# A two-layer macaron block on one core: later k products, weight blocks one a turn, a bias by a product, norms on VectorE at the joins

## The reference, cut to what matters

```python
def ffn0(x):                      # ternary weights
    h = relu(einsum('bsd,fd->bsf', x, quantize(W1)) + b1)       # width 512
    return einsum('bsf,df->bsd', h, quantize(W2)) + b2
def quantize(W):
    return clip(round(W / (mean(abs(W)) + 1e-5)), -1, 1)
def attn0(x):                     # 16 heads of 64
    x = rmsnorm(x, norm_w)
    sim = q k^T / 8 with q, k, v = heads of x Wq, x Wkv; causal mask
    out = softmax(sim) v
    return (sigmoid(x Wg) per head * out) Wout
def attn1(x):                     # the same with layernorm gamma, beta, a bias b_out, no gates
def moe(X):                       # 8 experts, the best 2 of each token
    topv, topi = top_k(X Wg + bg, 2); w = softmax(topv)
    out = X
    for j, e in the two: out += (silu((w_j X) W1[e]) * ((w_j X) W3[e])) W2[e]
    return out

# LN = layernorm over the 128 columns, eps 1e-5; every step reads the running x
x = x + 0.5 * ffn0(LN(x))
x = x + attn0(LN(x))
x = x + 0.5 * ffn0(LN(x))
x = x + 0.5 * moe(LN(x))
x = x + attn1(LN(x))
x = x + 0.5 * moe(LN(x))
```

## Time and profile before

| | us |
|---|---|
| time, median of 3 runs (range) | 1074.2 (1073.09 to 1074.45) |
| profiled execution, its own time | 1075.01 |
| its span, first to last instruction | 1073.2 |
| TensorE busy | 887.4 |
| VectorE busy | 809.5 |
| GpSimd busy | 715.8 |
| ScalarE busy | 626.4 |

### The profile page before, as it was taken

The page is one execution under the profiler, slowest core; times in us unless marked ns, Lnnn a source line. Parts: engine busy times, 40 slices in busy tenths (PEclk is TensorE's granted clock), DMA queues, the critical chain, the costliest instruction groups (busy, mean ns, idle before and its releaser), DMA issues.

```text
span 1073.2 us, 30778 instructions
## 1 busy us (share of the span) xinstructions
PE 887.4 (83%) x11870; PEld 617.3 (58%) x11870; DVE 809.5 (75%) x2348; ACT 626.4 (58%) x1036; POOL 715.8 (67%) x651
## 2 busy tenths in 40 slices
PE   3678999999999975279994699999999997359993
PEld 1445666666666653257772366666666665237772
DVE  4868988888888865757775887788787885567774
ACT  2749777776776742046653566676666664126661
POOL 5928888878777772067762587777776777037772
PEclk9779999999999996589997799999999999569997
DMA  4111111200000000011123000000000000011124
GB/s 143 40 40 41 41 41 41 81 3 12 2 2 13 2 2 11 10 40 54 53 44 86 2 2 2 2 13 2 2 13 2 2 12 2 10 25 51 53 53 133
DMA packets 29949, 31.74 MB, mean 30 GB/s; under 512 B 4657, under 2 KB 22833, under 8 KB 29809
## 3 DMA queue, kind: packets, MB, share of 16 engines
q1 hardware_dynamic: 23424, 19.41, 6.1%
q0 software_dynamic: 4992, 10.23, 3.7%
q10 hardware_dynamic: 1392, 0.14, 0.1%
HBM read 21.52 MB, written 8.26 MB: 28 GB/s over the span
## 4 chain that ended last, share of the span: by engine, by line
PE 55%; DVE 26%; issue 6%; POOL 5%; ACT 5%; DMA 2%; SPq 0%; DVEq 0%; POOLq 0%; ACTq 0%
PE ps L1539 8%; DVE arena L1118 6%; PE ps L1367 6%; PE ps L1368 6%; PE ps L1369 6%; PE ps L1562 3%; PE ps L1564 3%; PE ps L1563 3%; PE ps L1684 3%; PE ps L1545 3%; PE ps L1507 2%; ACT arena L836 2%; DVE arena L1007 2%; DVE arena L1141 2%; PE ps L1390 2%
## 5 line engine op out<-in xcount | busy, mean ns | idle before, releaser
L673 POOL TENSOR_TENSOR arena<-arena 128x1024 f16<-128x1024 f32 (+1 forms) x192 | 348.5, 1815 | 133.3 <-ACT arena L844 122.9
L836 ACT ACTIVATE arena<-ps 128x1024 f32<-128x1024 f32 (+1 forms) x192 | 169.4, 882 | 151.7 <-PE ps L1545 149.8
L1118 DVE CUSTOM_DVE_ANT_0 arena<-ps,mask_qk 128x512 bf16<-128x512 f32 (+3 forms) x512 | 224.1, 484 | 14.2 <-PE ps L1507 8.6
L1539 PE MATMUL ps<-arena 64*128 64x512 f16 (+3 forms) x1536 | 149.7, 301 | 24.6 <-ACT arena L836 21.3
L1562 PE MATMUL ps<-arena 128*128 128x65 f16 x1280 | 130.5, 195 | 3.8 <-POOL arena L673 3.8
L699 POOL DMA_INDIRECT arena<-x_rows,arena x78 | 76.5, 981 | 81.6 <-DVE arena L1290 53.4
L1563 PE MATMUL ps<-arena 128*128 128x64 f16 x1280 | 130.5, 193 | 0.0
L1564 PE MATMUL ps<-arena 128*128 128x65 f16 x1280 | 130.3, 194 | 0.0
L1562 PEld LDWEIGHTS ps<-arena 128*128 128x128 f16 x1280 | 118.6, 98 | 4.0 <-POOL arena L673 4.0
L1564 PEld LDWEIGHTS ps<-arena 128*128 128x128 f16 x1280 | 118.0, 98 | 0.0
L1563 PEld LDWEIGHTS ps<-arena 128*128 128x128 f16 x1280 | 117.9, 99 | 0.0
(11 more groups left out here) (251 smaller groups left out, 2628.2 us busy)
## 6 DMA issues: line engine op xcount, KB each, us to landing
stage<-in_L_ffn_W SPq DMA_DIRECT2D x4, 1024.0 KB, 5.5
arena<-y_rows SPq DMA_DIRECT2D x16, 256.0 KB, 4.9
x_rows<-XN SPq DMA_DIRECT2D x8, 256.0 KB, 2.3
arena<-x_rows,arena POOLq DMA_INDIRECT x78, 2.6
y_rows<-arena POOLq DMA_INDIRECT x78, 2.3
X<-in_L_attn_tokens SPq DMA_DIRECT2D x4, 256.0 KB, 7.0
stage<-in_L_attn_Wkv SPq DMA_DIRECT2D x2, 512.0 KB, 7.4
out_x<-X SPq DMA_DIRECT2D x4, 256.0 KB, 2.9
```

The source lines that it names most:

```text
L673: g.tensor_tensor(PL[:, b, :, cols], P32[:, :, cols], PH[:, b, :, cols], ALU.subtract).then_inc(s_pl, 1)
L836: a_.activation(P32[:, :, UNIT_AT[u]:UNIT_AT[u] + UNIT_W[u]], ps[:, 4:6, 0:UNIT_W[u]], ACT.Exp).then_inc(s_ex_p, 1)
L1118: v_.tensor_tensor_reduce(masked[:, x, 0:w], ps[:, 2 + x, at:at + w], mask_qk[:, CH - w:CH], 1.0, NEG, ALU.add, ALU.max, accum_out=MX[:, i ...
L1539: mm(ps[:, 4 + x, at:at + w], keys, queries, start=(n_ == 0 and part == 0), stop=False)
```

## The change

Five edits, given together:

1. In attention, k is projected behind the second unit's masks instead of behind q, in turns that have q and scores and no fill (`late_k`); its upper half on ScalarE and lower half on VectorE move with it.
2. Expert blocks go one a turn over turns 2 to 25; GpSimd makes all lower halves, ScalarE both copies.
3. The bias b1 enters the hidden block as a product: b1 in two float16 halves in rows 0 and 32 of `b1t`, the constant 1/64 in the same rows of `unit`. Relu then writes float16 directly from PSUM (ScalarE), and VectorE makes the lower half from PSUM as max(h, 0) - upper; GpSimd has no part. The float32 buffer for h goes.
4. `normed` of (2, 3), (3, 3), (4, 0) and (5, 3) is VectorE's (x - mean) x rstd; GpSimd leaves out `shift` for these.
5. The first feed-forward's order is new on all engines: token chunk 0 loads on ScalarE's queue, the small vectors on SP's; transposes of chunk c+1 stand in the middle of chunk c's ups; the second weight's ternary form comes after chunk 0; weight copies from PSUM are ScalarE's; masks and tables on GpSimd come later (`attention_masks`, `routing_tables`).

```diff
+        NORM_ON_DVE = ((2, 3), (3, 3), (4, 0), (5, 3))
         def quarters(t):
-            return (2 * t - 4, 2 * t - 3) if 2 <= t < 14 else ()
+            return (t - 2,) if 2 <= t < 26 else ()
+        def late_k(a, t):
+            p, m, s, v, o = items(t)
+            return p is not None and s is not None and not fill(a, t)[0]
...
@@ GpSimd
+            g.memset(unit[:], 0.0)
+            step(g.memset(b1t[:], 0.0))
+            step(g.memset(unit[0:1], 1.0 / W_UP))
+            g.memset(unit[32:33], 1.0 / W_UP).then_inc(s_b1_set, 1)
...
             for c in range(NCH):
                 rstd_of(0, c)
-                if c == 1:
-                    constants()
+            pool.wait_ge(s_small_in, 16 * 6)
+            step(g.tensor_scalar(b2h[:], b2h[:], 0.5, None, ALU.mult))
             base_add(0, 0, b2h[:])
+            attention_set()
             base_add(0, 1, b2h[:])
-            for c in range(NCH):
-                for k in range(FB):
-                    hidden_high(0, c, k)
...
+            rstd_of(1, 0)
+            base_add(0, 2, b2h[:])
+            attention_masks()
+            base_add(0, 3, b2h[:])
+            head_low(2)
@@ ScalarE
+            a_.dma_start(X[:, 0:TPC, :], tokens.rearrange("b (t p) d -> p (b t) d", p=P)[:, 0:TPC, :]).then_inc(s_x_in[0], 16)
+            for r in (0, 32):
+                a_.dma_start(T32[r:r + 1], ins["L0_ffn_b1"].rearrange("(a n) -> a n", a=1)).then_inc(s_b1_in, 16)
+            def hidden_high(f, c, k):
+                u, hi, _ = hidden(f, c, k)
                 act.wait_ge(s_up_ps, u + 1)
...
+                a_.activation(hi, ps[:, up_bank(f, c, k), :], ACT.Relu).then_inc(s_h_hi, 1)
+            normed(0, 0)
+            turned_x(0, 0)
+            ternary(0)
+            normed(0, 1)
+            for c in range(NCH):
+                hidden_high(0, c, 0)
+                hidden_high(0, c, 1)
+                if c < NCH - 1:
+                    turned_x(0, c + 1)
                 else:
+                    act.wait_ge(s_small_in, 16 * 6)
+                    turned_x(1, 0)
+                hidden_high(0, c, 2)
+                hidden_high(0, c, 3)
+                if c == 0:
+                    ternary(1)
+                if c < 2:
+                    normed(0, c + 2)
+                if c == 1:
+                    head_high(0)
+                if c == 2:
                     normed(1, 0)
+                    head_high(1)
...
                     if p is not None:
                         q_high()
-                        k_high()
+                        if not late_k(a, t):
+                            k_high()
...
                         exps(1)
+                        if late_k(a, t):
+                            k_high()
                         p_high()
@@ VectorE
+                v_.scalar_tensor_tensor(lo, ps[:, up_bank(f, c, k), :], 0.0, hi, ALU.max, ALU.subtract
+                                        ).then_inc(s_h_lo, 1)
+            def normed(n, c):
+                dve.wait_ge(s_ln_rstd, NORM_NO[n, c])
+                for t in range(TPC * c, TPC * (c + 1)):
+                    ins_ = v_.tensor_scalar(XN[:, t, :], X[:, t, :], mv[:, t, 0:1], rstd[:, t:t + 1], ALU.subtract,
+                                            ALU.mult)
+                ins_.then_inc(s_ln_xn, 1)
...
             for c in range(NCH):
+                hidden_low(0, c, 0)
+                hidden_low(0, c, 1)
+                turned_x(*((0, c + 1) if c < NCH - 1 else (1, 0)))
+                hidden_low(0, c, 2)
+                hidden_low(0, c, 3)
+                if c >= 1:
+                    x_ffn(0, c - 1)
                 if c == 1:
+                    stats(1, 0)
+                    head_low(0)
+                if c == 2:
                     head_low(1)
...
                     if m is not None:
                         maxima(2)
+                    if late_k(a, t):
+                        k_low()
                     if kind == "turn":
                         turned_x(n, c)
+                    if kind == "up":
+                        hidden_low(1, n, c)
@@ TensorE
             def up(f, c, k):
                 if f == 0 and u >= 4:
-                    pe.wait_ge(s_h_relu, u - 3)
-                mm(ps[:, bank, :], F1[:, k, :], XTh[:, c * CH:(c + 1) * CH], start=True, stop=False)
+                    pe.wait_ge(s_h_lo, u - 3)
+                mm(ps[:, bank, :].rearrange("p (a b) -> p a b", a=TPC), b1t[:, k, :],
+                   unit[:].unsqueeze(1).broadcast_to([P, TPC, P]), start=True, stop=False)
+                mm(ps[:, bank, :], F1[:, k, :], XTh[:, c * CH:(c + 1) * CH], start=False, stop=False)
...
             turned_x(0, 0)
-            turned_x(0, 1)
-            pe.wait_ge(s_f_got, 2)
+            ternary(0)
+            pe.wait_ge(s_b1_set, 3)
+            pe.wait_ge(s_f_got, 1)
             for c in range(NCH):
+                up(0, c, 0)
+                up(0, c, 1)
+                if c >= 1:
+                    pe.wait_ge(s_ln_lo, NORM_NO[0, c - 1])
+                if c < NCH - 1:
+                    turned_x(0, c + 1)
+                else:
+                    turned_x(1, 0)
+                up(0, c, 2)
+                up(0, c, 3)
+                if c == 0:
+                    ternary(1)
...
                     if p is not None:
                         project_q()
-                        project_k()
+                        if not late_k(a, t):
+                            project_k()
...
                         score_masks(1)
+                    if late_k(a, t):
+                        project_k()
                     if p is not None:
                         project_v()
```

More of the change, by code:

```diff
@@ L91, in macaron_block @@
         pw = sb("pw", [P, 2, NT], F32)
-        b1c = sb("b1c", [P, FB], F32)
+        b1t = sb("b1t", [P, FB, P], F16)
+        unit = sb("unit", [P, P], F16)
         b2h = sb("b2h", [P, D], F32)
@@ L503, in _ @@
             x_in = tokens.rearrange("b (t p) d -> p (b t) d", p=P)
-            for c in range(NCH):
+            for c in range(1, NCH):
                 sp.dma_start(X[:, TPC * c:TPC * (c + 1), :], x_in[:, TPC * c:TPC * (c + 1), :]).then_inc(s_x_in[c], 16)
+            for dst, src in small:
+                sp.dma_start(dst, src, allow_slow_non_contiguous=True).then_inc(s_small_in, 16)
             for i, (src, dst, _, _, _) in enumerate(heads):
@@ L606, in attention_set, with attention_masks @@
                 g.memset(VH, 1.0).then_inc(s_att_set, 1)
-            def constants():
-                step(g.memset(onesh[:], 1.0))
+            def attention_masks():
                 step(g.memset(sel[:], 0.0))
@@ L621, in constants, with routing_tables @@
                 step(g.tensor_copy(identb[:], ident[:]))
+            def routing_tables():
+                step(g.memset(onesh[:], 1.0))
+                g.affine_select(out=before[:], in_=onesh[:], pattern=[[1, P]], compare_op=ALU.is_gt, fill=0.0,
+                                base=0, channel_multiplier=-1)
                 g.iota(iota_e[:], pattern=[[0, NT], [1, EXPERTS]], base=0, channel_multiplier=0,
-                       allow_small_or_imprecise_dtypes=True)
-                g.iota(iota_t[:], pattern=[[1, ETILES], [0, EXPERTS]], base=0, channel_multiplier=0,
                        allow_small_or_imprecise_dtypes=True)
@@ L714, in _ @@
             base_add(2, 3, b2h[:])
-            for k in range(FB):
-                hidden_high(1, 3, k)
             rstd_of(3, 3)
@@ L805, in _ @@
[L805 to L821 removed]
+                a_.activation(hi, src, ACT.Copy, scale=W_UP)
@@ L895, in body @@
                     if kind == "up":
-                        relu(1, n, c)
+                        hidden_high(1, n, c)
                     if kind == "gate":
@@ L946, in _ @@
             for k in range(FB):
-                relu(1, 3, k)
-            normed(3, 3)
+                hidden_high(1, 3, k)
             turned_x(3, 3)
@@ L1045, in route, with ternary @@
                 step(ins_)
+            def ternary(k):
+                step(v_.tensor_scalar(f_low[:, k], f_in[:, k], fsm[:, k, 3:4], None, ALU.is_lt))
+                v_.scalar_tensor_tensor(f_in[:, k], f_in[:, k], fsm[:, k, 2:3], f_low[:, k], ALU.is_gt, ALU.subtract
+                                        ).then_inc(s_f_tern, 1)
+            stats(0, 0)
             dve.wait_ge(s_f_in, 32)
@@ L1060, in _ @@
-            for c in range(1, NCH):
-                stats(0, c)
-            for k, dst in enumerate((F1, F2)):
-                dve.wait_ge(s_f_tp, k + 1)
-                v_.tensor_copy(dst[:].rearrange("p a b -> p (a b)"), ps[:, 1 + 3 * k, :]).then_inc(s_f_got, 1)
+            step(v_.tensor_scalar(fsm[:, :, 1], ps[:, 0, 0:2], 1.0 / (DFF * D), 1e-5, ALU.mult, ALU.add))
+            v_.tensor_scalar(fsm[:, :, 2], fsm[:, :, 1], 0.5, None, ALU.mult)
+            step(v_.tensor_scalar(fsm[:, :, 3], fsm[:, :, 1], -0.5, None, ALU.mult))
@@ L1412, in _, with ternary @@
```

(2 more changed lines are left out.)

214 lines of the change are left out of this document (67 added, 147 removed).

## The result

| | before | after |
|---|---|---|
| time, median of 4 runs (range) | 1074.09 (1073.09 to 1074.45) | 1029.03 (1028.21 to 1029.85) |
| profiled execution: its own time, span | 1075.01, 1073.2 | 1028.21, 1026.4 |

The ratio is 0.9578, with the 95% interval 0.9565 to 0.9591: 45 us faster by the medians, 46.8 by the two profiled executions. The forecast was 1030 (1031.1 for the profiled execution).

What follows compares the result with a forecast made beforehand. No single bound: TensorE busy 83% of the span with 55% of the chain, VectorE 26%. Terms 11.6 + 6.5 - 2.5 + 3.7 + 2.4 + 17.5 + 4.7 = 43.9 off 1075.0 give 1031.1, less 0.8 for the median: 1030; range 1020 to 1046.

Steps and rivals of the forecast that it cites:

- k behind the second masks: Attention: moving k fills the second exponential's wait, saving 0.43 us in each of 27 turns, 11.6 us; bounds 0 and 12.5.
- the forecast's last sign: Attention stages: the forecast is wrong if the granted clock falls inside one of them.
- Blocks: First attention: weight blocks one a turn on GpSimd remove 0.54 us from turns 2 to 13, 6.5 us, less 2.5 charged.
- The charge of 2.5: First attention, turns 14 to 25: 2.5 us lost in three turns where norms and blocks meet; bounds 0 and 5.
- Ups: Attention's "up" turns: the bias product makes TensorE the bound at 9.64 us a turn, saving 3.7; bounds 0 and 6.
- turn 34: Feed-forward split done a turn earlier, so the stage's third "down" starts 2.4 us earlier; bounds 0 and 2.5.
- First stage: First feed-forward: new order starts q at 41 us, 17.5 us earlier, clock high after seven microseconds; bounds 6.5 and 21.5.
- The rival of the low clock: First feed-forward stays at the low clock: q starts at 52, 11 us later, total 1041; chance 0.13.
- Norms: Joins: four norms on VectorE at 0.6 us each save 4.7; bounds 2 and 6; (4,0) alone 0.5, from -0.8 to 1.6.
- Mixtures: Both mixture stages: no change in time forecast, 0 us.
- slower than before: Attention: TensorE at 100% is granted the lower clock in parts; at a tenth of the work, 1088 us; chance 0.03.
- GpSimd falling behind: Turns where norms and blocks meet: GpSimd falls behind, 1.5 us over ten turns; total 1055; chance 0.04.

Runs made afterwards that it cites:

- k_alone: Kernel before with the later k as its only edit: 1105.2 us, ratio 0.9919 to the kernel before.
- undo_k_blocks_norms: Kernel after with early k, two weight blocks a turn and the four norms on ScalarE again: 1091.37 us, ratio 0.9783 to the kernel before.
- after_again: The kernel after, unchanged, run again on the second group's chip: 1069.86 us, ratio 0.9598 to the kernel before.
- blocks_two: Kernel after with two weight blocks a turn in turns 2 to 13, the even one's lower half on VectorE: 1078.76 us, ratio 0.9681 to the kernel before.
- k_early: Kernel after with k projected behind q in all turns again: 1078.82 us, ratio 0.9673 to the kernel before.
- clears_first: Kernel after with GpSimd's two clears for attention 1 ahead of the statistics' root at (4, 0): 1069.11 us, ratio 0.9599 to the kernel before.
- no_bias: Kernel after without the bias product, b1 left out of the hidden layer: 1065.74 us, ratio 0.9549 to the kernel before.

## Why the prediction was right, point by point

The forecast held: 1030 against 1029.0, and 1031.1 against 1028.2 for the profiled execution, so the terms were 2.9 us short in sum. Some of them were right for the reason given. That the sum came so close is in part luck: the two attention stages gave 5.4 us more than their terms, the first stage 1.4 more; norms and mixtures took 2.7 and 2.0 back.

- **k behind the second masks, 11.6:** 10.4 by undoing it, without the first turns of attention 1 (9.0 by the medians), so 0.39 for each of the 27 turns and not 0.43. The first turns of attention 1 go with the clock and not with the change: turn 3 took 9.7 us in the four profiles in which the granted clock was back at 1.00 within 6.9 us of turn 2's copy of P, and 10.67 to 11.40 in the ten others, where it was back 13 to 17 us behind that copy. The first measurement had the kernel before among the ten and the kernel after among the four, 2.2 us over turns 2 to 4. By the letter of the forecast's last sign ("if the granted clock falls inside an attention stage") that fall speaks against it; it stands in the kernel before as well, and the ordinary turns behind it were all at 1.00. The ordinary turn was to be 8.99 and took 9.01, the full wait gone as the sum of TensorE's queue said, and the queued copy of P had its room. What failed was the assumption that the term stands by itself: with a block a turn on VectorE the same edit cost 1.2 us in attention 0 (k_alone).
- **Blocks, 6.5 less 2.5:** undoing them cost 10.9, for the same reason from the other side: it puts turns 7 to 11 at 10.45, not at 9.42 plus 0.54. With the early k they were worth 7.5. k and blocks together gave 9.6 + 8.6 = 18.2 (undo_k_blocks_norms against after_again) where I had 15.6. The charge of 2.5 for turns 14 to 25 found nothing: they took 116.5 us with a block each and 116.8 without (blocks_two). Turn 18 rose from 10.95 to 11.37 and the turn behind it fell from 10.3 to 9.41, but both did so in blocks_two as well: that is the late k in turn 19, and in k_early they were 10.90 and 10.10.
- **Ups, 3.7:** 4.5. The turn took 9.56 against 9.64, TensorE the bound as said. For turn 34, turns 34 and 35 gave 1.7 where the whole 2.4 was forecast: the last item's outputs then waited for GpSimd's lower half of P, which ended at 366.43. Behind that the join's "down" took 1.96 us, at the high level of the clock, instead of 3.58, which gave 1.6 that I had not counted; nothing in the change aims at it.
- **First stage, 17.5:** 18.9. First product at 12.81 (13.7), q's products from 39.62 (41), clock high from 17.5 (21). The rival of the low clock falls. The time was right and the way to it only in part: "without a break" and ScalarE as the bound are not what the trace shows. TensorE idled 3.8 of the 20.4 us to 37.4, it had nothing to do from 35.1 to the gate's products at 39.13, and VectorE had more of the chain than ScalarE.
- **Norms, 4.7:** 2.0, the term that was mis-sized. I took 0.6 for four instructions by the nearest row, 128x512 in one piece; in four pieces they took 1.12, 0.34 at best a piece. And that of (4,0) took 2.91 beside the clears, a gain of 0.5 that became a loss. I had given this mechanism the lower bound of -0.8 and not the value; the join lost 0.8 (0.5 by the medians over all kernels). By the rule that I cited of the Trainium skill ("SBUF — State Buffer", Who interferes with whom) it would be held; clears_first agrees: one instruction took 2.33 us behind the start of the clears, and 0.34 when they were done. (The sum that I worked out beside that rule, 3.3, should have been 3.4: 4.7 less 0.5 less 0.8.)
- **Mixtures, 0:** they took 2.0 us more. In the first one TensorE's clock rose 10.6 us behind its first gather (430.2 against 419.6), before 8.2 (466.1 against 457.9). The change has only a table of tile numbers replaced there; that the time of the clock's rise is the whole of it is argued, not shown.

The rival "slower than before" did not come: the granted clock was 1.00 with TensorE busy in 28.70 of 28.70 us. Nor did the one of GpSimd falling behind: the blocks of turns 14 to 25 cost nothing.

## What to carry to other kernels

Sum one engine's queue between the two waits that enclose it, and move work from the wait that is over-filled to the one that is not; for the ordinary turn such a sum held to 0.02 us, for the "up" turn to 0.08. Before pricing an edit, look which VectorE instructions of SBUF operands lie beside long GpSimd ones: half a microsecond of shift changed a 1.24 us split to 1.94 and undid part of another edit's gain. And price a small instruction by pieces of its own size, not by the same data in one piece.

## What the runs showed of the hardware that I had not expected

- A VectorE instruction over 128x16 took 2.00 us beside GpSimd's 2.12 over 128x1024, and 0.17 without it. Splitting 128x512 on VectorE took 0.66 at best, 1.24 mostly and up to 2.03; where I laid it beside GpSimd's subtraction (turn 8, above), it ended 0.55 behind it whenever it had started.
- Without the bias product, and so with less work for TensorE, the granted clock fell to 0.50 for 3.3 us at 30.6, behind a stretch where TensorE had been busy 10.40 of 13.50 us; with it, at 16.57 of 20.40 busy, it stayed at 1.00 to 37.4. That is one profile of no_bias against eleven of the others; that the missing product is the cause is likely, not shown.
- after and after_again are one program: its attention turns were the same to 0.01 us but for two, and its mixtures took 128 and 127 us in one measurement, 151 and 145 in the other (in each the first mixture, then the second). The runs don't say why.
